# Layer 3 of a fused four-layer GNN kernel: gathered halves as stationary operand, 38 dense and 11 gathered node tiles

## The reference, cut to what matters

```python
    deg_inv_sqrt = jnp.where(deg > 0, jax.lax.rsqrt(deg), 0.0)
    norm = deg_inv_sqrt[src] * deg_inv_sqrt[dst]
    def step(xk, _):
        msg = norm[:, None] * xk[src]
        agg = jax.ops.segment_sum(msg, dst, num_segments=n_nodes)
        return ((1.0 - ALPHA) * agg + ALPHA * h, None)
    xK, _ = jax.lax.scan(step, x, None, length=10)
    return jax.nn.relu(xK)
...
x = x + _L3_gnn_ref(h, edge_index)
```

## Time and profile before

| | |
|---|---|
| median of three runs | 5058.53 us |
| lowest, highest | 5050.29, 5061.18 us |
| the profiled execution | 5046.41 us |
| its span, first to last instruction | 5044.2 us |
| busy PE, DVE, ACT, POOL in the span | 86%, 53%, 20%, 64% |
| dense matmuls of layer 3 (L1954) | 9800 |
| gathers of layer 3 (L1005) | 1620 |

### The profile page before, as it was taken

How to read it: one execution, slowest core, us unless ns; L and a number is a source line. 1 busy time by engine, 2 the same in 40 slices (tenths; PEclk the granted TensorE clock), 3 DMA queues, 4 the chain that set the end, 5 groups by cost and what they waited for, 6 DMA issues and landing times.

```text
span 5044.2 us, 69350 instructions
## 1 busy us (share of the span) xinstructions
PE 4322.8 (86%) x24340; PEld 2811.4 (56%) x24340; DVE 2652.0 (53%) x8658; ACT 1022.2 (20%) x2892; POOL 3242.9 (64%) x3390
## 2 busy tenths in 40 slices
PE   3999589999884566666668999999999999999999
PEld 3776466676664555555554555555555555555554
DVE  7999445556544677778885333333232333332333
ACT  5887411111111001112232000000000000000001
POOL 2542377777776777777733767657575757575665
PEclk9999789999996766777779999999999999999999
DMA  5332322222222333333315666666666666666664
GB/s 150 111 114 94 84 66 71 70 71 66 71 71 75 97 95 96 95 95 92 90 48 167 195 194 193 194 195 198 187 202 192 195 193 196 191 198 189 189 203 152
DMA packets 456593, 686.27 MB, mean 136 GB/s; under 512 B 92897, under 2 KB 238983, under 8 KB 456224
## 3 DMA queue, kind: packets, MB, share of 16 engines
q1 hardware_dynamic: 342292, 454.72, 28.6%
q0 software_dynamic: 107584, 223.83, 17.0%
q10 hardware_dynamic: 6364, 3.20, 0.2%
HBM read 599.50 MB, written 82.31 MB: 135 GB/s over the span
## 4 chain that ended last, share of the span: by engine, by line
PE 50%; DVE 6%; POOL 5%; issue 2%; ACT 1%; DMA 0%; DVEq 0%; POOLq 0%
PE ps L1954 40%; POOL E L970 5%; PE pt L1984 5%; PE ps L1776 2%; DVE B L2483 1%; PE ps L1966 1%; DVE arena L2525 1%; PE pt L1784 1%; PE pt L1793 1%; PE ps L1903 0%; ACT C L1305 0%; DVE bn_st L2153 0%; DVE arena L2506 0%; ACT A L1305 0%; PE ps L1757 0%
## 5 line engine op out<-in xcount | busy, mean ns | idle before, releaser
L1005 POOL DMA_INDIRECT arena<-table,src_i x810 | 774.8, 957 | 497.5 <-DMA table<-E 252.1
L1954 PE MATMUL ps<-arena,E 128*128 128x512 fp8e4 (+1 forms) x4900 | 1077.8, 375 | 9.1 <-DVE C L2752 7.0
L1954 PE MATMUL ps<-arena,A 128*128 128x512 fp8e4 (+1 forms) x4900 | 1073.9, 374 | 0.0
L1005 POOL DMA_INDIRECT arena<-x_spill,src_i x810 | 773.3, 955 | 386.7 <-issue 227.7
L955 POOL DMA_INDIRECT arena<-table,src_i x782 | 741.3, 948 | 347.3 <-issue 236.2
L970 POOL DMA_INDIRECT E<-gat_table,src_i x782 | 762.1, 975 | 270.8 <-issue 235.1
L1699 PE MATMUL ps<-E,arena 128*128 128x352 f32 (+22 forms) x2932 | 737.7, 403 | 117.5 <-DMA arena<-table,src_i 116.7
L1954 PEld LDWEIGHTS ps<-arena,E 128*128 128x128 f16 x4900 | 480.3, 98 | 512.2 <-DVE C L2752 7.2
L1954 PEld LDWEIGHTS ps<-arena,A 128*128 128x128 f16 x4900 | 479.4, 98 | 499.2
L1699 PEld LDWEIGHTS ps<-E,arena 128*128 128x128 f32 x2932 | 492.1, 201 | 289.7 <-DMA arena<-table,src_i 139.7
L2403 DVE SCALAR_TENSOR_TENSOR E<-arena,pt 128x512 f32<-128x512 bf16 (+5 forms) x782 | 478.3, 674 | 23.2 <-PE ps L1699 22.5
(11 more groups left out here) (351 smaller groups left out, 4722.7 us busy)
## 6 DMA issues: line engine op xcount, KB each, us to landing
arena<-adj SPq DMA_DIRECT2D x180, 1024.0 KB
arena<-adj SPq DMA_DIRECT2D x90, 1088.0 KB
adj<-E SPq DMA_DIRECT2D x39, 784.0 KB, 3.6
arena<-table,src_i POOLq DMA_INDIRECT x1592
O<-dst_rows SPq DMA_DIRECT2D x112, 224.0 KB, 3.4
arena<-adj SPq DMA_DIRECT2D x20, 768.0 KB
arena<-x_spill,src_i POOLq DMA_INDIRECT x810
E<-gat_table,src_i POOLq DMA_INDIRECT x782, 2.9
```

The costliest lines, as they stand in the source:

```text
L1005: pool.indirect_dma_start(out=y_rows[:, g % ERING, k, :], out_offset=None, in_=(table, x_spill)[half], in_offset=bass.IndirectOffsetOnAxis ...
L1954: mm = pe.matmul(chunk_banks[n % 2][:, 0:len(some) * P], y[:, i, h * D:(h + 1) * D], adj_ring[:, piece % ADJ_RING, 0:len(some), at:at + P] ...
```

## The change

- POOLED goes from 10 to 11 and DENSE from 39 to 38. Adjacency is built, stored and streamed for 38 tiles; chunk 9 has two tiles in place of three. There are 178 edge tiles in 45 groups. LONG becomes 931 units.
- In the edge products the operands change sides. Each half of the gathered rows (128x128 f16) is stationary, and a narrow piece of one-hot is moving: only as many columns as node numbers the edge tile can reach, 2 to 60. The result has features on the partitions, like a dense chunk.
- The 11 gathered tiles form three chunks (38 to 41, 42 to 45, 46 to 48), each a bank of up to 512 columns, two banks by turns. A step has 190 parts of edge tiles, with two matmuls each: 380.
- Gathered chunks then take the way of the dense ones: copy by ScalarE, transposes, one VectorE instruction for each tile, store. `turn_of` numbers all 13 chunks of a step in the order of their transposes. A step has 13 stores in place of 20.
- The one-hots are made narrow, 206 instructions a step, cut where the iota of 256 columns wraps.
- EDGE_GAP goes from 21 to 20 and EDGE_LATE from 125 to 110. The last group is at 84 + 44 x 20 = 964, that is 33 units into the next step.

```diff
-POOLED = 10
+POOLED = 11
...
-TURN_LAG, STORE_LAG, EDGE_LAG, EDGE_LATE, EDGE_GAP = 10, 26, 84, 125, 21
+POOL_CHUNKS = (POOLED + CHUNK - 1) // CHUNK
+TURN_LAG, STORE_LAG, EDGE_LAG, EDGE_LATE, EDGE_GAP = 10, 26, 84, 110, 20
...
+        def pooled_parts(tile):
+            lo, hi = reach_of(tile)
+            lo, hi = max(lo, DENSE * P), (NP if tile == TILES - 1 else min(hi, NP))
+            ends = [lo, *range(DENSE * P + (lo // P - DENSE) // CHUNK * CHUNK * P + CHUNK * P, hi, CHUNK * P), hi]
+            return [((a // P - DENSE) // CHUNK, a, b) for a, b in zip(ends, ends[1:])]
+        def hot_parts(tile):
+            parts = pooled_parts(tile)
+            lo, hi = parts[0][1], parts[-1][2]
+            ends = [lo, *range(lo // (2 * P) * 2 * P + 2 * P, hi, 2 * P), hi]
+            return [(a - lo, b - lo, a % (2 * P)) for a, b in zip(ends, ends[1:])]
...
-            for i in range(DENSE, NT):
-                plan.append((first + EDGE_GAP * pooled_group(i), 3, "pooled", step, i, 0))
-                plan.append((first + EDGE_GAP * pooled_group(i) + STORE_LAG - TURN_LAG, 4, "store", step, i, i + 1))
+            for c in range(CHUNKS, CHUNKS + POOL_CHUNKS):
+                plan.append((first + EDGE_GAP * pooled_group(c), 3, "copy", step, c, 0))
+                plan.append((first + EDGE_GAP * pooled_group(c) + TURN_LAG, 1, "turn", step, c, 0))
+                plan.append((first + EDGE_GAP * pooled_group(c) + STORE_LAG, 4, "store", step, chunk_nodes(c).start, chunk_nodes(c).stop))
...
+                            if what < CHUNKS:
+                                n = step * CHUNKS + what
+                                act.wait_ge(sem("chunk_made"), n + 1)
+                                summed_up = chunk_banks[n % 2]
+                            else:
+                                n = step * POOL_CHUNKS + what - CHUNKS
+                                act.wait_ge(sem("multiplied"), n + 1)
+                                summed_up = edge_banks[n % 2]
...
-                                    mm = pe.matmul(edge_banks[i % 2][:, 0:2 * D], step_hot[(step * EGROUPS + g) % EHOT][:, k, i % 2 * P:(i % 2 + 1) * P],
-                                                   y_rows[:, r, k, :].bitcast(F16),
-                                                   start=(tile == first), stop=(tile == near_last[i]))
+                                for p, lo, hi in pooled_parts(tile):
+                                    nth, at = step * POOL_CHUNKS + p, (DENSE + p * CHUNK) * P
+                                    if tile == pooled_first[p] and nth >= 2:
+                                        pe.wait_ge(sem("turn_in"), turn_of[(nth - 2) // POOL_CHUNKS, CHUNKS + (nth - 2) % POOL_CHUNKS] + 1)
+                                    for h in range(2):
+                                        mm = pe.matmul(edge_banks[nth % 2][:, lo - at:hi - at], rows[:, h * D:(h + 1) * D],
+                                                       step_hot[(step * EGROUPS + g) % EHOT][:, k, lo - start_at:hi - start_at],
+                                                       start=(tile == pooled_first[p] and h == 0),
+                                                       stop=(tile == pooled_last[p] and h == 1), skip_group_check=True)
...
-                                a = dve.tensor_scalar(step_hot[nth % EHOT][:, k, :], iota_y, dst_f[:, at:at + 1], UNIT,
-                                                      ALU.is_equal, MUL)
+                                for lo, hi, near_by in hot_parts(at):
+                                    a = dve.tensor_scalar(step_hot[nth % EHOT][:, k, lo:hi], iota_y[:, near_by:near_by + hi - lo],
+                                                          dst_f[:, at:at + 1], UNIT, ALU.is_equal, MUL)
...
-                            dve.scalar_tensor_tensor(kept_part[:, CHUNK + 1, :], edge_banks[i % 2][:, 0:D], sc_b[:, i:i + 1],
-                                                     kept_part[:, CHUNK, :], MUL, ADD).then_inc(part_done, 1)
-                            dve.wait_ge(part_done, parts[0])
-                            dve.scalar_tensor_tensor(nodes(C)[:, i, :], edge_banks[i % 2][:, D:2 * D], sc_b[:, i:i + 1],
-                                                     kept_part[:, CHUNK + 1, :], MUL, ADD).then_inc(sem("y_tiles"), 1)
```

89 lines of the change are left out of this document (43 added, 46 removed).

## The result

The changed kernel takes 5114.1 us (median of four runs, 5104.1 to 5116.7) where the kernel before takes 5054.4 us (5047.0 to 5061.2). The ratio is 1.0115, with a 95% interval of 1.0093 to 1.0136: slower by 60 us, where 5060.5 us and a range of 5044 to 5092 had been forecast. The profiled executions have spans of 5112.9 and 5044.2 us. Chips differ: the kernel before took 5045 us and 5079 us (median) on two chips of the experiments and 6213 to 6283 us on four others, so each experiment is told as a ratio to the kernel before on its own chip.

A forecast was written before the change was run, and what follows sets the result against it. TensorE bound the kernel before; then the gathers' loop would, 223.0 + 10.7 = 233.7 us a step. With layer 0's 6.1 us gain the span came to 5046.2, 2.0 over 5044.2, or 5060.5 us by the median; range 5044 to 5092.

The forecast's parts named there:

- TensorE, term by term: Layer 3 step: dense, edge and transpose work sums to 224.9 us, some 9 less, with narrow matmuls 0.048 us apart.
- Rival D: Edge products: narrow matmuls dearer than 0.048 us, TensorE sets the step again; 5130 to 5150 or 5235 us; chance 0.1.
- The bound passes to the gathers' loop: Layer 3: the gathers' loop replaces TensorE as bound, at 233.7 us a step; 5060.5 us; chance 0.5.
- First to last gather, 223.0: GpSimd in a step: 178 gathers for 162, 16 x 1.25 = 20.0 us more, 223.0 us from first to last issue.
- VectorE and ScalarE ... priced at nothing: Layer 3 step: one-hots and copies cost nothing, as both engines are idle two thirds of a step.
- Landing, 2.9: Loop's close: the last gather lands after 2.9 us, the median of its kind; other end 5.99.
- Does TensorE keep up?: Step's end: TensorE reaches the last group before its rows land, with a margin of 2.2 to 5.3 us.
- Transposes to store and store to gather, 2.15 and 3.25: Loop's close: 2.15 us from transposes to the store's issue, then 3.25 us to the next step's first gather.
- Layer 0: VectorE-bound layer 0: one dense tile less and 16 more edge tiles gain 6.1 us, 3 to 9 as bounds.
- C: Rival: loop closes later; landings of 4.5 us add 1.6 us a loop, 5075 us; with 5.99, 5088; chance 0.2.
- The check that was named: GpSimd's gap between steps: about 10 us if right, 12 or more for C, below 9 if the loop closes sooner.
- 10.7: Step's end: us from last gather issue to next first gather, landing, matmuls, transposes and store in series.

The follow-up runs named there:

- e18: Changed kernel with half of the dense matmuls of the ten steps left out: 1.0014 of the kernel before, 236.9 us a step.
- e16: Changed kernel with the kept share made for one column in place of 128, the rest left out: 1.0038 of the kernel before.
- e17: Changed kernel with its groups of edge matmuls 19.3 units apart in place of 20: 5134.1 us, 1.0109 of the kernel before.
- Form alone: Changed kernel's narrow one-hots over gathered halves, with 10 gathered tiles and 162 gathers as before: 4981.5 us, 0.9873 of the kernel before.

## Why the prediction was wrong, point by point

- **TensorE, term by term: right in direction, and one price too high.** The forecast was 224.9 us of work; the window has 221.4. The narrow matmuls stand 0.025 us apart (3426.46 0.10 x4), not 0.048. With that price the sum is 216. Of the 5 us up to 221.4, 1.7 are the stretch at half the clock, and an estimated 3 to 4 the restarts: behind a wait the way of the first matmul through the array is counted as busy time, 0.2 us (3415.48 0.40 x8 against 3421.94 0.19 x8; from the group's start to that of the next dense matmul it is 0.22 and 0.21 us), and TensorE stops 15 to 19 times a step. Rival D has fallen. Its 81 ns from the Trainium skill ("TensorE: Matmul & The Clock Gate", section "Back-to-back issue gap") is the page's figure for 128 moving columns, and was the wrong one to take: for up to 64 the page gives a floor of about 25 ns, and the trace agrees, with 128 weight columns and up to 60 moving ones.
- **The bound passes to the gathers' loop: right.** The chain of work of the changed kernel and the step of e18, 237 us with TensorE idle for a third of it, both show it.
- **First to last gather, 223.0: too small by 2.7 us.** The step added 16 x 1.25 to what the kernel before had, and took over that kernel's small excess of gathers behind VectorE. With the new order no more gathers start inside the kept share's bursts, but more of them at places where they wait (42 over 1.2 us in ten steps, for 6). "VectorE and ScalarE ... priced at nothing" is the sentence that failed: VectorE's busy share was low, but it was on the loop by way of GpSimd. e16 shows it: without the kept share's work the gathers' excess is gone.
- **Landing, 2.9: too small by 2.05 us.** The bounds (2.9 to 5.99) held the value, 4.95; the choice of the median failed, since the loop closes where loads of the adjacency are in flight. In seven of eight loops TensorE came later still, so that the landing that cost was the one of the third-last group. e18 leaves the last one where it is, and there it is on the path.
- **"Does TensorE keep up?": failed.** I compared TensorE's arrival at the last group with the last rows' landing and found a margin of 2.2 to 5.3 us. But TensorE does not run through to that point: it stops 15 to 19 times in a step for rows, in the step shown for the last time at the third-last group, and from that landing on (3415.43) it has 46 dense matmuls and two transposes to do, 11 us, while the last rows land 7.4 us on (the last gather at 3417.59, its rows 5.2 us later). A sum of work over a whole step hides that; what counts is the work behind the last wait. e18 takes 1.4 us off that term with half of the dense matmuls gone.
- **Transposes to store and store to gather, 2.15 and 3.25: right** (2.19 and 3.05).
- **Layer 0: right, and given back.** VectorE's stretch of layer 0 ends at 479.4 us for 486.6 before, 7.2 us sooner (forecast 6.1). The first gather of layer 3 is only 2.8 us earlier (2710.86 for 2713.69). Three more traces of the same program up to there, on another chip (e16, e17, e18), have 2706.1, 2724.4 and 2727.1, so a few microseconds can't be followed through the layers between.
- **The rivals.** C was the case: the loop closes later. Its price, 1.6 us a loop for landings of 4.5, was close for the landing alone; it knew neither the kept share nor the dense matmuls behind the last wait. Together 6.8 us times nine are 62 us, against the 15 to 28 of C. The clock did fall at the new waits, as C named: nine times in steps two to nine the granted clock was 0.50, once for 6.8 us and eight times for 3.4, where the kernel before has 1.00 in all of these steps. The eight stand right behind a wait of TensorE of 1.9 to 2.8 us. In the middle of a step it costs nothing that shows: step seven, with two of them, takes 239.4 us, and step five, with none, 240.5. Behind the last wait, as in the step shown, it is on the path and costs some 1.5 us (10.8 us from the third-last group to the last one, for 9.3).
- **The check that was named** would have told it: a gap of GpSimd between steps of 12 us or more was to mean C; it is 12.3 to 15.7 us (12.59 at 3191.55).

The whole: TensorE's gain of 12 us a step, and room for more, was bought with 16 gathers, 20 us, which is all the slack that the loop had (233.6 - 202.9 - 10.7 = 20.0 by the prediction's own terms). From there each small term of a chain in series counted nine times. Form alone keeps TensorE's gain and leaves the loop its slack.

## What to carry to other kernels

When a change moves the bound from an engine to a loop through memory, every term of that loop is in series and is multiplied by its count: price the transfers at its close with the load that stands around them, not with the median of all, and price the compute engine from its last wait on, not over the whole step. Ask of an idle vector engine whether it can still hold up the engine on the path. And where a change has two parts, one that lightens the engine at the bound and one that moves work to another, try the first alone: here it gives 1.3%, and the two together lose 1.2% (on chips of the faster kind; on the others it gives nothing).

## What the runs showed of the hardware

- f16 matmuls with fresh weights of 128 columns and up to 60 moving columns stand 0.025 us apart (four in 0.10 us), about half of the 0.048 us worked out from four of 48 columns in bf16 in layer 2.
- A gather's issue on GpSimd (0.95 us) that starts inside a burst of four f32 operations with two SBUF inputs on VectorE (1.13 us together) takes up to 1.95 us, 1.25 us on average in the changed kernel; with the burst's operations cut to one column the excess is gone (e16: 0.94 us on average).
- The arrival of a group's gathers (64 KB each) is signalled 2.6 to 2.7 us after the last one's start in the median where the queue of SyncE fills under 0.1 of the DMA engines' time, and 4.7 to 5.0 us after it where it fills over 0.7.
- TensorE's granted clock fell to 0.50 for 3.4 us eight times in the changed kernel's steps two to nine, each time right behind a wait of 1.9 to 2.8 us; in the kernel before, without such waits, it stayed at 1.00. The mean of a step, 0.99, does not show it.
- On four of six chips of the experiments the same program takes 24% longer, with instructions of TensorE that start 0.7 us or multiples of it apart while waiting for nothing that the profile shows; a change that gains 1.3% on one kind of chip gains nothing on the other.
